# Loading the per-subject bias b0 straight into the tile that is added, with the landing counted by SyncE

## What is computed

```python
x = x + einsum('bnh,boh->bno', x, W0[subject]) + b0[subject]      # 8 subjects
x = x + rotate(x, delta_t, amplitudes, frequencies)               # pairs of tokens
x = x + einsum('bsd,bdh->bsh', x, W2[category]) + b2[category]    # 64 categories
h = relu(x @ W1[language] + b1[language])                         # 9 of 10 languages
y = x + h @ Wup[language] + bup[language]
x = x + layernorm(y) * gamma[language] + beta[language]
```

## Time and profile before

| | |
|---|---|
| three executions | 1143.76, 1144.45, 1145.31 us; median 1144.45 |
| the profiled execution | 1143.54 us, with a span of 1141.1 us in the profile |
| TensorE | busy 1102.6 us, 97% of the span; granted clock 0.99 in the mean |
| TensorE's weight loads | 924.0 us, beside the products |
| VectorE | 916.4 us, 80% |
| ScalarE | 778.7 us, 68% |
| GpSimd | 677.9 us, 59% |
| transfers | 353.5 MB, 310 GB/s in the mean; SyncE's queue busy 86.7% of 16 engines' span |
| chain that ended last | TensorE 92%, VectorE 2%, issue 2%, ScalarE, DMA and GpSimd 1% each |

### The profile page before, as it was taken

How to read it: one execution, slowest core, us unless ns; L and a number is a source line. 1 busy time by engine, 2 the same in 40 slices (tenths; PEclk the granted TensorE clock), 3 DMA queues, 4 the chain that set the end, 5 groups by cost and what they waited for, 6 DMA issues and landing times.

```text
span 1141.1 us, 28378 instructions
## 1 busy us (share of the span) xinstructions
PE 1102.6 (97%) x6046; PEld 924.0 (81%) x6046; DVE 916.4 (80%) x1373; ACT 778.7 (68%) x1824; POOL 677.9 (59%) x807
## 2 busy tenths in 40 slices
PE   4799999999999999999999999999999999999996
PEld 2588888888788888888888888887888888787885
DVE  7787787778987787778978877878877878888876
ACT  3476776767676776767767666767767767676764
POOL 5756556557755656556656556566556566565563
PEclk9899999999999999999999999999999999999999
DMA  7898979897998999799989889988998999798882
GB/s 247 307 330 302 321 284 334 315 309 277 381 338 295 322 316 315 269 351 327 333 303 361 307 275 341 323 300 308 356 310 286 342 316 356 263 369 323 312 297 70
DMA packets 97554, 353.50 MB, mean 310 GB/s; under 512 B 11870, under 2 KB 12510, under 8 KB 79932
## 3 DMA queue, kind: packets, MB, share of 16 engines
q1 hardware_dynamic: 95756, 350.39, 86.7%
q10 hardware_dynamic: 1584, 0.93, 0.3%
HBM read 316.94 MB, written 34.34 MB: 308 GB/s over the span
## 4 chain that ended last, share of the span: by engine, by line
PE 92%; DVE 2%; issue 2%; ACT 1%; DMA 1%; POOL 1%; DVEq 0%; SPq 0%; POOLq 0%; ACTq 0%
PE ps_mix L1075 10%; PE ps_l L1064 10%; PE ps_l L1100 10%; PE ps_l L1048 10%; PE ps_l L1094 10%; PE ps_l L1090 10%; PE ps_hT L1120 9%; PE ps_l L1059 5%; PE ps_x3T L1110 5%; PE ps_l L1052 5%; PE ps_y L1133 3%; PE ps_y L1131 3%; PE ps_y L1130 3%; DVE w_lo L873 1%; DMA x_in<-xT 1%
## 5 line engine op out<-in xcount | busy, mean ns | idle before, releaser
L595 ACT ACTIVATE w_hi<-w_in 128x1024 fp32r<-128x1024 f32 x256 | 270.8, 1058 | 219.5 <-POOL w_in L469 219.5
L873 DVE TENSOR_TENSOR w_lo<-w_in,w_hi 128x1024 fp32r<-128x1024 f32 x256 | 333.7, 1303 | 19.8 <-ACT w_hi L595 18.1
L482 POOL TENSOR_SCALAR var_eps<-square_sum 128x1 f32<-128x1 f32 x128 | 24.4, 191 | 414.5 <-DVE w_lo L873 307.9
L902 DVE TENSOR_TENSOR x<-ps_l,rows 128x512 f32<-128x512 f32 x126 | 87.0, 691 | 124.3 <-PE ps_l L1100 124.3
L640 ACT ACTIVATE x3T<-ps_x3T,minus_bup 128x128 f32<-128x128 f32 x512 | 145.8, 366 | 49.3 <-PE ps_x3T L1110 48.0
L508 POOL TENSOR_TENSOR x_beta<-x,rows 128x512 f32<-128x512 f32 x128 | 168.8, 1319 | 0.0
L476 POOL TENSOR_TENSOR x_lo<-x_in,x_hi 128x512 fp32r<-128x512 f32 x127 | 164.1, 1292 | 7.5 <-ACT x_hi L571 7.5
L469 POOL TENSOR_TENSOR w_in<-w_in,ident 128x512 f32<-128x512 f32 x128 | 166.5, 1301 | 2.9 <-DMA w_in<-W 2.9
L1075 PEld LDWEIGHTS ps_mix<-mix,x 128*128 128x128 f32 x1024 | 125.0, 192 | 32.9 <-issue 32.8
L1048 PE MATMUL ps_l<-w_hi,x_hi 128*128 128x512 f32 x512 | 150.2, 415 | 0.0
L1075 PE MATMUL ps_mix<-mix,x 128*128 128x128 f32 x1024 | 141.9, 282 | 4.9 <-DVE x L883 4.9
(11 more groups left out here) (148 smaller groups left out, 1843.7 us busy)
## 6 DMA issues: line engine op xcount, KB each, us to landing
w_in<-W SPq DMA_DIRECT2D x128, 1024.0 KB, 6.6
rows<-sample_rows SPq DMA_DIRECT2D x128, 768.0 KB, 7.1
x_in<-xT SPq DMA_DIRECT2D x128, 256.0 KB, 6.2
w_in<-W SPq DMA_DIRECT2D x128, 256.0 KB, 5.0
out<-yb SPq DMA_DIRECT2D x128, 256.0 KB, 6.6
w_in<-W0T SPq DMA_DIRECT2D x7, 1024.0 KB, 5.5
wup_sb<-Wup SPq DMA_DIRECT2D x1, 2560.0 KB, 13.7
w_in<-W0T SPq DMA_DIRECT2D x4, 512.0 KB, 6.4
```

The lines of the kernel that those rows point to most:

```text
L595: act.activation(w2_hi[:, halves[n]], w2_in[s % WB][:, halves[n]], ACT.Copy).then_inc(w2_hi_made, 1)
L873: dve.tensor_tensor(w2_lo[:, half], w2_in[s % WB][:, half], w2_hi[:, half].bitcast(fp32), ALU.subtract).then_inc(w2_lo_made, 1)
```

## The change

b0 no longer has landing tiles. SyncE loads it straight into `b0_sb`, from which x1 reads, in a function of its own that is called in every turn behind the load of W1: for a new subject, three positions ahead, it waits for x1 of two places before, issues the DMA, waits for its landing, and increments `b0_renewed` (which nothing reads). With or without a new subject it increments `b0_landed` in each turn, and VectorE waits for that count before x1. W0's landing semaphore now counts 16 for each load instead of 32. GpSimd's copy, `b0_in` and `b0_made` are gone. `in_two_turns` holds for positions 20 to 101 instead of 18 to 109.

```diff
-        b0_in = [sb(f"b0_in{i}", [P, D]) for i in range(2)]
...
-        b0_made = [sem(f"b0_made{i}") for i in range(2)]
+        b0_renewed = sem("b0_renewed")
+        b0_landed = sem("b0_landed")
...
             for e in range(2):
                 sp.sem_inc(w0_lo_made[e], 2)
-                sp.sem_inc(w0_loaded[e], 32)
-                sp.sem_inc(b0_made[e], 2)
+                sp.sem_inc(w0_loaded[e], 16)
...
                     sub, ordinal = subject_of(sp, s), ordinal_of(sp, s)
                     sp.wait_ge(w0_lo_made[e], 2 * ordinal)
-                    sp.wait_ge(b0_made[e], ordinal)
                     sp.dma_start(w0_in[e][:, :], W0T[bass.ds(sub, 1)].rearrange("o p c d -> p (o c d)"))\
                         .then_inc(w0_loaded[e], 16)
-                    sp.dma_start(b0_in[e][:, :], b0[bass.ds(sub, 1)].rearrange("o d -> (o d)").partition_broadcast(P))\
-                        .then_inc(w0_loaded[e], 16)
+
+            def load_b0(s, j):
+
+                e = j % 2
+                first = is_first(sp, s)
+                with sp.If(first):
+                    sub, ordinal = subject_of(sp, s), ordinal_of(sp, s)
+                    sp.wait_ge(x1_made, s - 1)
+                    sp.dma_start(b0_sb[e][:, :], b0[bass.ds(sub, 1)].rearrange("o d -> (o d)").partition_broadcast(P))\
+                        .then_inc(b0_loaded[e], 16)
+                    sp.wait_ge(b0_loaded[e], 16 * ordinal)
+                    sp.sem_inc(b0_renewed, 1)
+                sp.sem_inc(b0_landed, 1)
...
             for s in range(2, 5):
                 load_w0(s, s)
+            load_b0(2, 2)
...
                 if 0 < k < LAST - 1:
                     load_w1(s + 2, k + 2, j + 2)
 
+                if k < LAST - 2:
+                    load_b0(s + 3, j + 3)
                 if k < LAST - 4:
                     load_w0(s + 5, j + 5)
...
-                    pool.wait_ge(w0_loaded[e], 32 * ordinal)
+                    pool.wait_ge(w0_loaded[e], 16 * ordinal)
                     pool.tensor_tensor(diagonal_of(w0_in[e]), diagonal_of(w0_in[e]),
                                        ident[:, :].unsqueeze(1).broadcast_to([P, C, P]), ALU.add).then_inc(w0_folded[e], 2)
-                    pool.wait_ge(x1_made, s - 1)
-                    pool.tensor_copy(b0_sb[e][:, :], b0_in[e][:, :]).then_inc(b0_made[e], 1)
...
                 if s < 2:
                     dve.wait_ge(b0_loaded[s], 16)
+                else:
+                    dve.wait_ge(b0_landed, s - 1)
                 dve.wait_ge(l0_done, s + 1)
...
-                return 18 <= s < 110
+                return 20 <= s < 102
```

## The result

Four executions of the changed kernel took 1182.49 to 1191.09 us, 1188.07 in the median; the kernel before beside it took 1144.88. The ratio is 1.0371, with a 95% interval of 1.0354 to 1.0387: 43 us slower. The forecast was 1183, in a range of 1157 to 1204.

The account below looks back on a forecast made before the run. SyncE, not busy TensorE, would become the bound: its demand of 801.5 us (turns, loop ends, W0, b0) exceeds 753.6 by 47.9; less the spare, 39 us are added to 1143.5, giving 1183 against the median, range 1157 to 1204.

Parts of the forecast that it names:

- Rival A: SyncE becomes the bound of the whole kernel: 1183 us, own range 1165 to 1200; chance 0.60.
- Term 1: SyncE's added value load, branch and increment behind W1 in every turn: 0.98 us, raising its turn from 7.07 to 8.05.
- Term 2: SyncE's new block in seven b0 turns, waiting for a landing taken as 5.3 us: 6.9 us each.
- The loop's ends: Extra time from W1 to W2 at SyncE's seven twelve-turn loop ends: 3.8 us each in the mean, 26.6 in all.
- Term 4: GpSimd loses seven copies, 11.3 us in all, that nobody waits for: gain taken as 0, at most 11.3 us.
- Term 5: VectorE's wait for the landing count before x1 in every turn, already met and covered by its pipeline: taken as 0.
- the stretch: The 89 turns from W1 at 286.49 to W1 at 1040.11, 753.6 us before, over which SyncE's demand is summed.
- The spare: How late SyncE may issue the bias rows before VectorE's L902 must wait for them: 8.85 us.
- Rival B: SyncE catches up between single subjects, only the pair at positions 30 and 31 is paid: 1152 us; chance 0.12.
- both bounds: Sum's uncertainty: per-turn cost (0.88 to 1.1 us), 9 us per tenth; landing (2.65 to 7.9 us), -18 to +18.
- Rival C: More than the block is lost, by loop-body fetches, landings at 7.9 us or TensorE's clock: 1195 us; chance 0.18.
- Rivals D and E: D: SyncE's waits absorb additions, freed GpSimd helps DVE, 1133 to 1142; E: no change, 1142.2 to 1146.7; chance 0.05 each.

## Why the prediction was right

**The bound (right).** Rival A, given 0.60, is what happened: from position 28 on, up to 1093.66 us, SyncE's demand sets the time, and the stops show as VectorE's wait for the bias rows and ScalarE's for x. At positions 30 and 31 the delay of x1 grew by 7.6 us, where the forecast had some 10.

**Term 1, the If (right in size, by two errors that cancel).** The forecast took 7.07 us, one of the shortest turns, and added 0.98. The mean of the 19 plain turns before in which W1 followed the store within 1.6 us, so with no wait, is 7.34, and a plain turn after takes 8.10. W1 to W2 did grow by 0.95; the turn as a whole by 0.76. The sum needs only the 8.05 that came out as 8.10, and that it came out so near is luck.

**Term 2, the blocking wait (right in kind, 14% too large).** The landing took 3.1 to 5.7 us, 4.4 in the median, and not 5.3, which was taken from transfers that stood behind 1 MB. SyncE's wait for it, 3.9 us in the mean, is just under the 4 to 7 named as a sign. The block cost 5.96 us instead of 6.9, so 6.6 us of the sum were too much.

**The loop's ends (too small).** They cost 4.86 us instead of 3.8, so 7.4 us too little; this and the 6.6 us too much of term 2 nearly cancel, which is luck too. (The 3.8 is the mean of all seven ends before; the two in the earlier trace rows alone give 3.5.)

**Term 4, the copy (right).** No gain from it shows in the run in which ScalarE issues the load.

**Term 5, VectorE's wait (wrong).** Taken as 0, it is 3.7 us by itself. It didn't spoil the sum, for where SyncE's demand sets the time it isn't paid; moved out of the way, it gave nothing back. Only in the quiet turns before position 28 does it show, about 1 us of the 2.0 by which the stretch begins later.

**The spare (right).** 8.85 us was the forecast; SyncE ends the stretch 8.1 us later than TensorE does.

**The working on paper.** Three readings in the forecast are off, and none moves the 1183. Rival B's terms as written add to 16.2 us; about 8 comes out only with the 8.85 us of spare taken off, which the text doesn't say. Its single subjects are not at least 9 turns apart: 110 and 117 are 7 apart. And the lower ends of both bounds together, -9 and -18 us, reach 1156, not 1150.

**Rival B (0.12)** fell by the rate: with 0.3 to 0.4 us a turn SyncE never caught up between subjects. **Rival C (0.18)** named TensorE's clock. It did fall, in four short stretches that begin near 310, 610, 836 and 1040 us, each behind a stop of VectorE and TensorE for the bias rows (2.3 us the first, 4.8 to 5.7 the others); the first of them is in these rows of the changed kernel (columns as in the earlier trace rows). From 302 to 308 us TensorE is busy for 3.66 of 6 us, and from 312 to 314 the granted clock is 0.50, the lower of its two levels (1.2 GHz, where 1.00 is 2.4):

```profile
302.00:308.00 6.00, 3.66 (x15) 2.17 (x14) 3.68 (x6) 1.95 (x3) 3.94 (x6) 1.00 0.90 308
308.00:316.00 8.00, 6.74 (x32) 5.95 (x33) 5.44 (x9) 4.12 (x11) 1.12 (x2) 0.79 0.48 163
```

```profile
312.00:314.00 2.00, 2.00 (x11) 2.00 (x11) 0.78 (x2) 1.54 (x2) 0.00 (x0) 0.50 0.82 213
```

But SyncE didn't wait for TensorE once in the stretch, so what the slower clock cost TensorE didn't lengthen it. The forecast says that the row at 53.90 of the kernel before agrees with what it cites on waits for transfers. It does so only in part: the clock fell behind a stop, but that stop ended with VectorE's split of Wup:

```profile
53.72 0.63 PE L1130 MATMUL ps_y<-wup_hi,h_hi 128*128 x1 [4.50 <-DVE wup_sb L907]
```

**Rivals D and E (0.05 each)** fell with the time: the change is neither faster nor the same.

## What to carry to other kernels

An engine that issues transfers has two numbers, how late it may be and how fast it makes up time, and neither is in a table of busy times: read the first as landing to use, the second as its wait in a quiet turn. Work in every turn takes from the rate, a blocking wait takes from the store, and only what exceeds both is paid; so two edits that are cheap alone can be dear together: 10.6 and 6.2 us alone, 42.6 together. Put rare work inside a branch that an engine has already, and a wait that is always met where the engine waits anyway.

## What the runs showed that I hadn't expected

A wait that has long been met cost VectorE 0.04 us a turn when it stood just before the instruction that TensorE needs next (3.7 us in all), and nothing measurable at the head of `finish_l2`, where VectorE waits anyway. And a loop's end took SyncE 4.2 to 5.5 us more in the changed kernel than the same stretch of a plain turn (7.45 to 8.75 us, less 3.27); with 24 turns in the body in place of 12, 26.5 us came back.
